# First attention: where GpSimd builds the second half's gate tables

## The chip, the cores and the metric

The kernel runs on one core of a Trainium2 chip. The metric is the device time of one execution in microseconds (us), smaller is better; the median of three runs is given.

## The reference, cut to what matters

The program is a two-layer block over 16 sequences (B) of 128 tokens (N) with 256 features. Layer 0 is a cross attention with 16 heads of 64 whose scores are weighted by a gate computed from boxes, then a ternary feed-forward layer. Layer 1 is a second cross attention, then a mixture of 8 experts with two experts per token. Only the first attention matters here:

```
emb = box_relational_embedding(boxes)            # sin and cos of 4 log distances x 2 frequencies
g   = relu(einsum('bnmd,hd->bhnm', emb, Wg) + bg)
a   = einsum('bhqd,bhkd->bhqk', q, k) / sqrt(64)
mn  = softmax(log(clip(g, 1e-6)) + a)
x   = x + tanh(g_xattn[0]) * (einsum('bhqk,bhkd->bqhd', mn, v) @ Wo.T + bo)
```

The x and y distances need a logarithm per pair of tokens (the "features"). The width and height distances are differences of logarithms, so their sines and cosines separate into a part of the query token times a part of the key token: those parts are the "gate tables".

## The kernel before, in words

All matmul operands are pairs of float16, a high half (rounded) and a low half (the rest), so that three products give nearly float32 results. ScalarE writes most high halves, GpSimd (POOL) most low halves by a subtraction, VectorE (DVE) does what reads PSUM.

The first attention is one loop over the 16 sequences, written out by hand for each engine as `iteration(b, ...)`, with semaphores between the engines. In iteration b each engine works on several sequences: the scores and gate of b, the projections of b + 1, the probability-times-value product, turn and output projection of b - 1, and the loads and split of b + 2. The order on an engine is the order in which its program is written; a wait holds everything behind it on that engine.

- **VectorE**, in iteration b: `norm` (L862) of b + 2; `row_max` (L873) and `take_qk` (L894); `take_pv` (L886); `feature_floor` (L846), `take_v` (L903), `feature_turns` (L851), `xn_low` (L867); `residual` (L909, L912); `feature_fractions` (L855, L857); `feature_distance` of b + 2 (L839, eight instructions, the last of which raises `s_fd`, called gate_difference, to b + 3); `probs` (L923, eight instructions: gate times exponentials into PT); and `bn_stats` (L1012).
- **ScalarE**: `probs_high` of b - 1 (L1419, four instructions, after all of `probs`), conversions, the logarithm (L1355), `take_o` (L1377), the negated expert weights (L1383), the exponentials (L1393), and the sine and its high half (L1362, L1366).
- **GpSimd**: `half_low(b - 1)` (L573, a DMA with accumulation that waits for ScalarE's L1383), `probs_low(b - 1)` (L560, four instructions, each after one of L1419), `feature_low` (L555), `split_qk` (L546, four), `half_high` (L569, a DMA), `split_v` (L551, two), `split_ctx` (L516, "the context's low half") and then, in some iterations, `separable`.
- **TensorE**: its product of probabilities and values (`pv`, L1766) waits for all four L560; later it turns the result, and `project_o` (L1786, float32) waits for L1377.
- **SyncE** queues the loads. At b = 8 `store_tables(1)` (L378, L379) waits for all eight GpSimd tables of the second half, writes them to DRAM and waits for that; `load_tables` (L388) reads a sequence's tables back.

`separable(g, j, base)` builds table part j (16 query tokens) of half g: two multiplications into Lp (L521), then a sum to float16 (L526), a sum in place (L528) and a subtraction (L530). Each of the last three waits for the one before it through `s_pp` (prefix_pool), and the helper ends with a wait for L530. Half 0 (sequences 0 to 7) is built before the loop. Half 1 is needed from sequence 8 on; before the change its eight parts are built at the end of iterations 0 (parts 0 and 1) and 1 to 6 (part b + 1).

Of the kernel before, what the change touches and what calls it, by code (L numbers as in the profile page):

```python
# [25 lines left out]
NJ = N // NN  # L26
# [43 lines left out]
def build(nc, a):  # L70
    with ExitStack() as ctx:
        def sem(name):
            return ctx.enter_context(nc.semaphore(name))
# [206 lines left out]
        s_fd, s_fv, s_fa, s_fhi, s_flo = (sem("gate_" + n) for n in ("difference", "vector", "scalar", "high", "low"))  # L280
# [11 lines left out]
        s_ts, s_tl = sem("tables_stored"), [sem("tables_loaded_even"), sem("tables_loaded_odd")]  # L292
# [211 lines left out]
        def _(gp):  # L504
            pc = Count(s_pp)
# [7 lines left out]
            def split_ctx(b, par):  # L513

                gp.wait_ge(s_ch, b + 1)
                nc.gpsimd.tensor_tensor(ctx16[:, par, 1, :, :], ctxf[:, par, :, :], ctx16[:, par, 0, :, :], ALU.subtract).then_inc(s_cl, 1)  # L516

            def separable(g, j, base):

                for r in range(2):  # L520
                    nc.gpsimd.tensor_tensor(Lp[:, r, :, :], AB[:, r, :].unsqueeze(2).to_broadcast([P, H, NN]),  # L521
                                            wht[:, r, g:g + 1, bass.ds(j * NN, NN)].to_broadcast([P, H, NN]), ALU.mult).then_inc(s_pp, 1)
                gp.wait_ge(s_pp, base + 2)
                high = Lw16[:, 0, bass.ds(j, 1), :].rearrange("p o (h n) -> p (o h) n", h=H)
                low = Lw16[:, 1, bass.ds(j, 1), :].rearrange("p o (h n) -> p (o h) n", h=H)
                nc.gpsimd.tensor_tensor(high, Lp[:, 0, :, :], Lp[:, 1, :, :], ALU.add).then_inc(s_pp, 1)  # L526
                gp.wait_ge(s_pp, base + 3)
                nc.gpsimd.tensor_tensor(Lp[:, 0, :, :], Lp[:, 0, :, :], Lp[:, 1, :, :], ALU.add).then_inc(s_pp, 1)  # L528
                gp.wait_ge(s_pp, base + 4)
                nc.gpsimd.tensor_tensor(low, Lp[:, 0, :, :], high, ALU.subtract).then_inc(s_pp, 1)  # L530
                gp.wait_ge(s_pp, base + 5)
# [9 lines left out]
            def split_qk(b, par):  # L541
                for r in range(4):
                    w, g = r // 2, r % 2
                    hi = q16[:, par, w, 0, HS * g:HS * g + HS, :]
                    gp.wait_ge(s_qh, 4 * b + r + 1)
                    nc.gpsimd.tensor_tensor(q16[:, par, w, 1, HS * g:HS * g + HS, :], qt[:, r, :, :], hi, ALU.subtract).then_inc(s_ql, 1)  # L546

            def split_v(b, par):
                for r in range(2):
                    gp.wait_ge(s_vh, 2 * b + r + 1)  # L550
                    nc.gpsimd.tensor_tensor(vv16[:, par, 1, 8 * r:8 * r + 8, 0:DK], vf[:, r, :, :], vv16[:, par, 0, 8 * r:8 * r + 8, 0:DK], ALU.subtract).then_inc(s_vl, 1)  # L551

            def feature_low(n, par):
                gp.wait_ge(s_fhi, n + 1)
                nc.gpsimd.tensor_tensor(F16s[:, par, 1, :], fs, F16s[:, par, 0, :], ALU.subtract).then_inc(s_flo, 1)  # L555

            def probs_low(c):
                for g in range(4):
                    gp.wait_ge(s_ph, 4 * c + g + 1)
                    nc.gpsimd.tensor_tensor(PT16[:, 1, HS * g:HS * g + HS, :], PT[:, HS * g:HS * g + HS, :],  # L560
                                            PT16[:, 0, HS * g:HS * g + HS, :], ALU.subtract).then_inc(s_pl, 1)

            def half_expert(h):
                return a["wcat"][h // 2, :, (h % 2) * HC:(h % 2 + 1) * HC]

            def half_high(h):
                if h > 1:
                    gp.wait_ge(w_ld[h % 2], h // 2 * 16)
                gp.dma_start(w16_dram.ap()[h // 2, :, 0, (h % 2) * HC:(h % 2 + 1) * HC], half_expert(h)).then_inc(w_hi[h % 2], 16)  # L569

            def half_low(h):
                gp.wait_ge(w_ng, h * NSP + NSP)
                gp.dma_start(wsp[:, h % 2, :], half_expert(h), accum_op=ALU.add, max_dma_last_dim=6144).then_inc(w_lo[h % 2], 16)  # L573
# [7 lines left out]
            def iteration(b, par, c, has_q, has_x, has_s=False):  # L581
                if c:
                    half_low(b - 1)
                    probs_low(b - 1)
                    feature_low(b, par)
                if has_q:
                    split_qk(b + 1, 1 - par)
                if has_x:
                    half_high(b + 2)
                if has_q:  # L590
                    split_v(b + 1, 1 - par)
                if has_x:
                    split_ctx(b + 2, par)
                if has_s:

                    if b == 0:
                        gp.wait_ge(s_ts, 96)
                        separable(1, 0, pc.n + 5 * NJ)
                    separable(1, b + 1, (b + 1) * 5 + (pc.n + 5 * NJ))

            iteration(0, 0, 0, True, True, True)

            iteration(1, 1, 1, True, True, True)
            for b in range(2, B - 2):
                iteration(b, b % 2, 2, True, True, b < NJ - 1)
            iteration(B - 2, 0, 2, True, False)
            iteration(B - 1, 1, 2, False, False)
            half_low(B - 1)
# [1613 lines left out]
```

## Time and profile before

| | us |
|---|---|
| median of 3 runs | 1168.07 |
| lowest and highest run | 1168.0 and 1172.73 |
| the profiled execution's own time | 1164.61 |
| its span (first to last instruction) | 1162.8 |
| mean granted TensorE clock, share of full speed | 0.925 |
| busy: PE / DVE / ACT / POOL | 955.3 / 836.2 / 689.7 / 718.9 |

The four engines are all busy for 59 to 82% of the span, and no one of them is the limit throughout: the chain of work that ended last runs through PE (51%), DVE (18%), POOL (14%) and ACT (6%). Shares of the whole span say nothing of one stage, so the first attention (until about 490 us) has to be read in its own stretch.

### The profile page before, as it was taken

How to read it: one execution, taken by the hardware profiler on the slowest of the kernel's cores; microseconds unless marked ns; L12 is line 12 of the kernel's file. 1: busy time of each engine (PE TensorE's matmuls, PEld its weight loads, DVE VectorE, ACT ScalarE, POOL GpSimd, SP SyncE). 2: the span in 40 equal slices, each digit the busy share in tenths (PEclk: the TensorE clock that was granted, in tenths of full speed). 3: DMA queues.
4: the chain of work that ended last, by engine and by line, in shares of the span. 5: the costliest groups of instructions: out<-in, count | busy, mean ns of one | idle time of the engine just before them, and what ended most of it. 6: DMA issues, size and time to landing. Idle time of an engine off the chain costs nothing.

```text
span 1162.8 us, 32870 instructions
## 1 busy us (share of the span) xinstructions
PE 955.3 (82%) x12178; PEld 779.8 (67%) x12178; DVE 836.2 (72%) x1947; ACT 689.7 (59%) x1338; POOL 718.9 (62%) x811
## 2 busy tenths in 40 slices
PE   0448988899999996387878559995599999999996
PEld 0336766667777764364554248873599999999995
DVE  3997888877887775657776779985566666666663
ACT  2456878888888884145425548884354545454542
POOL 2988778886677752115341539984566766666663
PEclk9888999999999997669999869995799999999998
DMA  9276667678776756330001000000555215841251
GB/s 277 72 192 142 122 129 146 150 167 183 140 149 154 154 105 148 98 130 1 1 14 41 19 2 16 26 21 19 201 142 140 32 32 140 246 142 32 32 144 16
DMA packets 52118, 119.65 MB, mean 103 GB/s; under 512 B 7617, under 2 KB 30145, under 8 KB 51633
## 3 DMA queue, kind: packets, MB, share of 16 engines
q0 software_dynamic: 14144, 35.48, 21.3%
q1 hardware_dynamic: 35520, 80.71, 20.7%
q10 hardware_dynamic: 2352, 2.10, 0.6%
q8 instruction: 66, 1.08, 0.4%
q14 instruction: 36, 0.29, 0.1%
HBM read 212.54 MB, written 37.85 MB: 215 GB/s over the span
## 4 chain that ended last, share of the span: by engine, by line
PE 51%; DVE 18%; POOL 14%; ACT 6%; issue 5%; DMA 4%; POOLq 0%; ACTq 0%; SPq 0%; DVEq 0%
PE bank L2107 17%; PE bank L2121 9%; POOL PT L560 6%; PE bank L1786 6%; PE bank L1689 3%; PE bank L1766 2%; DVE nmx L1177 2%; ACT EX L1393 2%; PE bank L1728 2%; DVE h L1063 2%; PE bank L1937 2%; PE bank L1721 1%; DVE PT L923 1%; PE bank L1780 1%; DMA gates<-in_g_ffn 1%
## 5 line engine op out<-in xcount | busy, mean ns | idle before, releaser
L1623 ACT ACTIVATE yg<-bank,bms 128x128 f32<-128x128 f32 x312 | 107.8, 364 | 106.8 <-PE bank L2107 98.9
L1296 DVE TENSOR_TENSOR hm<-hf,hm 128x256 f16<-128x256 f32 x156 | 70.3, 450 | 81.5 <-ACT hm L1630 81.5
L1291 DVE SCALAR_TENSOR_TENSOR hf<-bank,bms,yg 128x128 f32<-128x128 f32 x312 | 98.1, 345 | 33.2 <-ACT yg L1623 32.0
L2107 PE MATMUL bank<-xT,wm_even 128*128 128x128 f16 x1920 | 115.6, 221 | 1.0 <-DVE xT L1303 1.0
L2107 PEld LDWEIGHTS bank<-xT,wm_even 128*128 128x128 f16 x1920 | 111.5, 99 | 2.1 <-DVE xT L1303 1.4
L560 POOL TENSOR_TENSOR PT<-PT 128x512 f16<-128x512 f32 x64 | 72.7, 1183 | 61.4 <-ACT PT L1419 61.4
L707 POOL DMA_INDIRECT out_x<-ys,sidx x39 | 62.8, 1611 | 76.2 <-DVE ys L1310 76.2
L2107 PE MATMUL bank<-xT,wm_odd 128*128 128x128 f16 x1824 | 108.0, 219 | 1.8 <-DMA wm_odd<-expert_weights 1.8
L2107 PEld LDWEIGHTS bank<-xT,wm_odd 128*128 128x128 f16 x1824 | 104.2, 98 | 2.4 <-issue 1.9
L1630 ACT ACTIVATE hm<-hf 128x256 f16<-128x256 f32 x156 | 64.5, 414 | 63.1 <-DVE hf L1291 61.7
L619 POOL TENSOR_TENSOR h<-h 128x512 f16<-128x512 f32 x32 | 40.6, 1281 | 83.0 <-DVE h L1063 81.0
L546 POOL TENSOR_TENSOR q<-qt,q 128x512 f16<-128x512 f32 x64 | 80.0, 1299 | 0.8 <-ACT q L1406 0.7
L666 POOL TENSOR_TENSOR P<-P 128x512 f16<-128x512 f32 x64 | 72.9, 1171 | 11.4 <-ACT P L1579 11.4
L1786 PE MATMUL bank<-WoT,OT 128*128 128x256 f32 x256 | 64.5, 409 | 1.9 <-ACT OT L1377 1.9
L700 POOL DMA_INDIRECT xin<-expert_tokens,gidx x39 | 42.0, 1076 | 31.1 <-POOL b2r L722 25.5
L1786 PEld LDWEIGHTS bank<-WoT,OT 128*128 128x128 f32 x256 | 50.9, 204 | 13.3 <-ACT OT L1377 6.1
L1406 ACT ACTIVATE q<-qt 128x512 f16<-128x512 f32 x64 | 38.8, 625 | 33.8 <-DVE qt L894 33.8
L2121 PE MATMUL bank<-wm_even,hm 128*128 128x256 f16 x480 | 55.7, 273 | 2.0 <-DVE hm L1296 2.0
L717 POOL TENSOR_SCALAR gts<-xin,etf 128x1 f32<-128x1 f32 x78 | 56.3, 1091 | 0.7 <-DMA xin<-expert_tokens,gidx 0.6
L1766 PE MATMUL bank<-vv,PT 128*128 128x65 f16 x768 | 33.9, 200 | 26.4 <-POOL PT L560 15.6
L1747 PE MATMUL bank<-We,F16s 128*128 128x256 f16 x384 | 53.7, 276 | 0.0
L1689 PE MATMUL bank<-wqkv,ctx 128*128 128x512 f16 x192 | 48.1, 390 | 6.4 <-DVE qt L894 6.4
(308 smaller groups left out, 2646.7 us busy)
## 6 DMA issues: line engine op xcount, KB each, us to landing
wm_even<-expert_weights SPq DMA_DIRECT2D x60, 1024.0 KB
wm_odd<-expert_weights SPq DMA_DIRECT2D x57, 1024.0 KB
expert_weights<-in_wcat POOLq DMA_DIRECT2D x16, 768.0 KB, 7.8
wsp<-expert_weights SPq DMA_DIRECT2D x16, 768.0 KB, 4.4
wsp<-in_wcat POOLq DMA_DIRECT2D x16, 768.0 KB, 10.3
expert_weights<-wsp SPq DMA_DIRECT2D x16, 768.0 KB, 3.3
Lst<-gate_tables SPq DMA_DIRECT2D x48, 68.0 KB, 6.0
gate_tables<-Lw SPq DMA_DIRECT2D x6, 512.0 KB, 3.3
```

The costliest lines, as they stand in the source:

```text
L546: nc.gpsimd.tensor_tensor(q16[:, par, w, 1, HS * g:HS * g + HS, :], qt[:, r, :, :], hi, ALU.subtract).then_inc(s_ql, 1)
L560: nc.gpsimd.tensor_tensor(PT16[:, 1, HS * g:HS * g + HS, :], PT[:, HS * g:HS * g + HS, :], PT16[:, 0, HS * g:HS * g + HS, :], ALU.subtract ...
L666: nc.gpsimd.tensor_tensor(P116[:, b % 2, 1, HS * g:HS * g + HS, :], P1[:, b % 2, HS * g:HS * g + HS, :], P116[:, b % 2, 0, HS * g:HS * g + ...
L707: nc.gpsimd.indirect_dma_start(out=a["out"], out_offset=bass.IndirectOffsetOnAxis(ap=sidx[:, t:t + 1], axis=0), in_=ys[:, t % 2, :], in_of ...
L1291: v.scalar_tensor_tensor(hf[:, (c // 2) % 2, c % 2, :], bank[c % 4][:, MT:2 * MT], bms[:, par, FC + c:FC + c + 1], yg[:, c % 4, :], ALU.ad ...
L1296: v.tensor_tensor(hm16[:, par, 1, c - 1:c + 1, :], hf[:, q % 2, :, :], hm16[:, par, 0, c - 1:c + 1, :], ALU.subtract).then_inc(m_hl, 1)
L1623: s.activation(yg[:, c % 4, :], bank[c % 4][:, 0:MT], ACT.Gelu, bias=bms[:, par, c:c + 1]).then_inc(m_g, 1)
L1630: s.activation(hm16[:, par, 0, 2 * q:2 * q + 2, :], hf[:, q % 2, :, :], ACT.Copy).then_inc(m_hh, 1)
L1689: ins = t.matmul(bank[2 + r][:, :], ctx16[:, par, xp, kk, :], wqkv16[:, 2, wp, kk, 512 * r:512 * r + 512], start=(n == 0), stop=(n == 5))
L1786: ins = t.matmul(bank[7][:, 0:D], OT[:, ch, :], WoT[:, ch, :], start=(ch == 0), stop=(ch == CH - 1))
L2107: ins = t.matmul(bank[c % 4][:, w * MT:(w + 1) * MT], wm16[par][:, wp, col:col + P], xT16[:, par, xp * KD + kk, :], start=(n == 0), stop=( ...
L2121: ins = t.matmul(bank[5 + par][:, 0:D], hm16[:, par, xp, c, :], wm16[par][:, wp, col:col + D], start=(n == 0), stop=(n == 3 * FC - 1))
```

## The change

Table part b of the second half is now built in iteration b, not in iteration b - 1. In GpSimd's program it stands after `half_low(b - 1)` and before `probs_low(b - 1)`, and waits for `s_fd` to reach b + 2, which is VectorE's last `feature_distance` instruction of its iteration b - 1. Part 0 stays at the end of iteration 0. Nothing else is changed.

```diff
             def iteration(b, par, c, has_q, has_x, has_s=False):
                 if c:
                     half_low(b - 1)
+                    if has_s:
+                        gp.wait_ge(s_fd, b + 2)
+                        separable(1, b, b * 5 + (pc.n + 5 * NJ))
                     probs_low(b - 1)
                     feature_low(b, par)
...
                 if has_x:
                     split_ctx(b + 2, par)
-                if has_s:
-
-                    if b == 0:
-                        gp.wait_ge(s_ts, 96)
-                        separable(1, 0, pc.n + 5 * NJ)
-                    separable(1, b + 1, (b + 1) * 5 + (pc.n + 5 * NJ))
+                if has_s and b == 0:
+                    gp.wait_ge(s_ts, 96)
+                    separable(1, 0, pc.n + 5 * NJ)
...
             for b in range(2, B - 2):
-                iteration(b, b % 2, 2, True, True, b < NJ - 1)
+                iteration(b, b % 2, 2, True, True, b < NJ)
```

The instructions of PE, DVE, ACT and SP are the same and in the same order; only GpSimd's differ. At its border between iterations 0 and 1 (the first five rows removed are table part 1):

```order
-L521 TENSOR_TENSOR Lp<-AB,wht 128x256 [waits prefix_pool]
-L521 TENSOR_TENSOR Lp<-AB,wht 128x256
-L526 TENSOR_TENSOR Lw<-Lp 128x256 [waits prefix_pool]
-L528 TENSOR_TENSOR Lp<-Lp 128x256 [waits prefix_pool]
-L530 TENSOR_TENSOR Lw<-Lp,Lw 128x256 [waits prefix_pool]
 L573 DMA wsp<-in_wcat 128x2x1536 [waits half_expert_negated,prefix_pool]
-L560 TENSOR_TENSOR PT<-PT 128x512 [waits probs_high] x4
+L521 TENSOR_TENSOR Lp<-AB,wht 128x256 [waits gate_difference]
+L521 TENSOR_TENSOR Lp<-AB,wht 128x256
+L526 TENSOR_TENSOR Lw<-Lp 128x256 [waits prefix_pool]
+L528 TENSOR_TENSOR Lp<-Lp 128x256 [waits prefix_pool]
+L530 TENSOR_TENSOR Lw<-Lp,Lw 128x256 [waits prefix_pool]
```

The part moved from in front of the DMA L573 to behind it, and L560 now follows L530 instead of the DMA. At the later borders (iterations 1 to 6 into the next) GpSimd had before:

```order
L516 TENSOR_TENSOR ctx<-ctxf,ctx 128x256 [waits ctx_high]
L521 TENSOR_TENSOR Lp<-AB,wht 128x256 x2
L526 TENSOR_TENSOR Lw<-Lp 128x256 [waits prefix_pool]
L528 TENSOR_TENSOR Lp<-Lp 128x256 [waits prefix_pool]
L530 TENSOR_TENSOR Lw<-Lp,Lw 128x256 [waits prefix_pool]
L573 DMA wsp<-in_wcat 128x2x1536 [waits half_expert_negated,prefix_pool]
L560 TENSOR_TENSOR PT<-PT 128x512 [waits probs_high] x4
```

and has now:

```order
L516 TENSOR_TENSOR ctx<-ctxf,ctx 128x256 [waits ctx_high]
L573 DMA wsp<-in_wcat 128x2x1536 [waits half_expert_negated]
L521 TENSOR_TENSOR Lp<-AB,wht 128x256 [waits gate_difference]
L521 TENSOR_TENSOR Lp<-AB,wht 128x256
L526 TENSOR_TENSOR Lw<-Lp 128x256 [waits prefix_pool]
L528 TENSOR_TENSOR Lp<-Lp 128x256 [waits prefix_pool]
L530 TENSOR_TENSOR Lw<-Lp,Lw 128x256 [waits prefix_pool]
L560 TENSOR_TENSOR PT<-PT 128x512 [waits probs_high,prefix_pool]
L560 TENSOR_TENSOR PT<-PT 128x512 [waits probs_high] x3
```

Each part stands one DMA and one wait on VectorE later, directly ahead of the low halves of the probabilities; iteration 7, which built none before, now builds the last one.

## Rows read from the trace of the kernel before

**Rows 1.** The page's costliest groups: busy us, mean ns, then idle before.

```profile
L560 POOL TENSOR_TENSOR PT<-PT 128x512 f16<-128x512 f32 x64 | 72.7, 1183 | 61.4 <-ACT PT L1419 61.4
```

**Rows 2.** Windows from one L560 group's start to the next: length, busy, clock, DMA.

```profile
95.94:124.56 28.62, 23.33 (x277) 17.48 (x275) 20.83 (x43) 18.93 (x28) 19.17 (x21) 0.94 0.69 127
124.56:149.66 25.10, 23.40 (x309) 18.02 (x306) 20.27 (x44) 20.37 (x30) 20.79 (x19) 1.00 0.69 139
...
250.04:273.64 23.60, 21.79 (x279) 16.39 (x277) 19.26 (x45) 20.39 (x30) 16.26 (x14) 1.00 0.87 195
```

**Rows 3.** Timeline of VectorE, a 25.1 us iteration: start, length, instruction.

```profile
214.97 1.35 DVE L912 SCALAR_TENSOR_TENSOR X<-otmp,tg,X 128x256 f32<-128x256 f32 x1
...
221.46 2.73 DVE L923 SCALAR_TENSOR_TENSOR PT<-bank,EX 128x256 f32<-128x256 f32 x8
```

**Rows 4.** Timeline of GpSimd in the same iteration.

```profile
214.83 1.20 POOL L521 TENSOR_TENSOR Lp<-AB,wht 128x256 f32<-128x256 f32 x2
...
216.98 1.06 POOL L528 TENSOR_TENSOR Lp<-Lp 128x256 f32<-128x256 f32 x1
218.12 1.53 POOL L530 TENSOR_TENSOR Lw<-Lp,Lw 128x256 f16<-128x256 f32 x1
```

**Rows 5.** Timeline of VectorE in a 23.6 us iteration, which builds no table.

```profile
312.37 0.49 DVE L912 SCALAR_TENSOR_TENSOR X<-otmp,tg,X 128x256 f32<-128x256 f32 x1
...
316.87 2.74 DVE L923 SCALAR_TENSOR_TENSOR PT<-bank,EX 128x256 f32<-128x256 f32 x8
...
319.87 0.40 DVE L862 TENSOR_SCALAR xn<-X,mv,rstd 128x256 f32<-128x256 f32 x1
```

**Rows 6.** Timeline of GpSimd and ScalarE in the same iteration.

```profile
315.46 1.21 POOL L573 DMA_DIRECT2D wsp<-in_wcat  x1 [3.17 <-ACT wsp L1383]
320.15 1.13 ACT L1419 ACTIVATE PT<-PT 128x512 f16<-128x512 f32 x2
320.85 1.15 POOL L560 TENSOR_TENSOR PT<-PT 128x512 f16<-128x512 f32 x1 [4.19 <-ACT PT L1419]
```

**Rows 7.** Timeline of GpSimd at the border between iterations 0 and 1.

```profile
90.77 1.20 POOL L521 TENSOR_TENSOR Lp<-AB,wht 128x256 f32<-128x256 f32 x2
...
93.66 0.67 POOL L530 TENSOR_TENSOR Lw<-Lp,Lw 128x256 f16<-128x256 f32 x1
94.64 1.30 POOL L573 DMA_DIRECT2D wsp<-in_wcat  x1 [0.31 <-POOL Lw L530]
```

**Rows 8.** Timeline of VectorE at the same border.

```profile
90.69 2.07 DVE L923 SCALAR_TENSOR_TENSOR PT<-bank,EX 128x256 f32<-128x256 f32 x6
...
93.70 0.79 DVE L862 TENSOR_SCALAR xn<-X,mv,rstd 128x256 f32<-128x256 f32 x1
```

**Rows 9.** Timelines of VectorE and TensorE in iteration 1.

```profile
103.49 4.05 DVE L846 TENSOR_SCALAR fu<-fu 128x1024 f32<-128x1024 f32 x1
...
110.17 5.41 PE L1786 MATMUL bank<-WoT,OT 128*128 128x256 f32 x16
```

**Rows 10.** The same two instructions in a 23.6 us iteration.

```profile
304.78 0.74 DVE L846 TENSOR_SCALAR fu<-fu 128x1024 f32<-128x1024 f32 x1
...
308.15 3.72 PE L1786 MATMUL bank<-WoT,OT 128*128 128x256 f32 x16
```

**Rows 11.** Windows of iteration 1: columns as in rows 2.

```profile
105.00:110.00 5.00, 1.58 (x9) 0.59 (x6) 4.47 (x4) 2.43 (x4) 3.40 (x4) 1.00 0.73 206
110.00:115.00 5.00, 5.00 (x17) 3.96 (x16) 0.42 (x1) 4.29 (x7) 4.58 (x7) 0.66 1.00 264
```

**Rows 12.** Timeline of GpSimd before the loop, right behind table part 7 of half 0.

```profile
61.52 0.68 POOL L530 TENSOR_TENSOR Lw<-Lp,Lw 128x256 f16<-128x256 f32 x1
62.28 4.48 POOL L546 TENSOR_TENSOR q<-qt,q 128x512 f16<-128x512 f32 x4
```

**Rows 13.** Timeline of SyncE's queue: the stored tables and the first load.

```profile
244.78 0.33 SPq L378 DMA_DIRECT2D gate_tables<-Lw  x1
...
258.49 1.25 SPq L388 DMA_DIRECT2D Lst<-gate_tables  x3
```

## The prediction

> **What bounds the kernel now.** I read the page first. Its costliest groups say that GpSimd sat idle for 61.4 us ahead of L560, released by ScalarE's L1419 [rows 1]. So in the first attention GpSimd, over the loop, has time to spare, yet L560 is what TensorE's product of probabilities and values waits for. Its first instruction in each iteration is a good beat to count by. Second, I cut the loop into windows from beat to beat [rows 2]. There are three lengths: 28.62 us for iteration 1, then 25.10 five times over (the first is shown), then 23.60 from 250 us on. DVE is busy 20.27 us in a long one and 19.26 in a short one, and POOL 20.79 against 16.26. The long ones are those in which a gate table was built (five of them, after iteration 1). PE, ACT and the clock differ little, so the 1.50 us are no work of TensorE.
>
> Third, I set the timelines of a long and a short iteration side by side. In the long one VectorE needs 221.46 - 214.97 = 6.49 us from L912 to the start of L923 [rows 3]; in the short one 316.87 - 312.37 = 4.50 us [rows 5]. That is 1.99 us, and it begins with L912, 1.35 us in place of 0.49. It has inputs in SBUF and runs beside GpSimd's L521, whose last table step takes 1.53 us here [rows 4] and 0.67 elsewhere [rows 7]. Each engine holds the other up. L923 then starts late, L1419 waits for it, and L560 waits for L1419. In the short iteration VectorE's L923 ends before ScalarE is free (319.6 against 320.15) [rows 5, 6]: 0.5 us of the 1.99 had cover, and 1.5 show.
>
> **The change part by part.** *The old place is emptied.* In the five long iterations nothing of GpSimd runs beside L912 to L839, so they become short ones: 5 x (25.10 - 23.60) = 7.5 us. That is the firmest term, since the kernel itself shows the short iteration [rows 2].
>
> *The new place.* Seven tables (parts 1 to 7) now run behind L573 and behind the end of L839. In a short iteration L573 ends at 315.46 + 1.21 = 316.67, and L839 at the start of L923, 316.87 [rows 5, 6]. POOL's answer to a semaphore takes about 0.1 us, so a table starts at 316.97. Undisturbed it takes 93.66 + 0.67 - 90.77 = 3.56 us [rows 7] and ends at 320.53; the next instruction follows 0.08 us behind such an end [rows 12]. That is 320.61, and L560 starts at 320.85 anyway [rows 6]. It fits with 0.24 us to spare. L573 itself is issued earlier than in a long iteration and costs nothing: it ends ahead of the wait.
>
> What runs beside it? L923 first. Does it collide as L912 does? The border of iterations 0 and 1 already has this very pair: table part 1 at 90.77 beside L923 at 90.69 [rows 7, 8]. Six L923 take 2.07 us there, 0.33 from start to start, as do the eight in 2.74 [rows 5], and the table steps are at their shortest. So I take zero. The upper bound is the rate of the old place, 218.12 + 1.53 - 214.83 = 4.82 us for a table [rows 4]: 1.26 us more, of which 0.24 are covered, so 1.0 per iteration and 7 us in all. After L923 comes `norm` (L862, 319.87), which does collide: 0.79 us behind the same table against 0.40 [rows 5, 8]. If VectorE wins there, GpSimd's last step starts up to 0.4 late, L560 0.15 late, and seven times that is 1 us. If GpSimd wins, `norm` is 0.4 late, and its followers have slack because TensorE waits for L560. I take 0.3 us in all, between 0 and 1.
>
> The Trainium skill ("SBUF — State Buffer", Who interferes with whom) says that VectorE and GpSimd share a pair of ports under an exclusive lock, that a float32 `tensor_scalar` from SBUF to SBUF takes it, and that whoever issues first keeps it for its whole instruction. It speaks against this place: `norm` would hold the table up each time, and the sum would be that 1 us worse, no more.
>
> *Iteration 1.* This is the term that the reader may miss. Its 28.62 us hold two more delays: L846 takes 4.05 us against 0.74, and L1786 5.41 against 3.72 [rows 9, 10]. L846 starts 7.55 us after the beat (103.49 - 95.94), exactly as in the short iteration (304.78 - 297.25 = 7.53, that beat being 23.60 ahead of 320.85) [rows 6, 10], so it is not late; it is held 3.31 us by GpSimd's L546, running without a gap. Before it GpSimd ran from the DMA L573 straight into L560, with no wait between them: the DMA ends at 94.64 + 1.30 = 95.94, the beat [rows 7, 2]. Its queue ran ahead and stayed ahead. In the later iterations L560 begins after an idle wait [rows 6], and L846 gets through. Now L573 is followed by the table, whose steps wait for each other, and L560 starts behind a real wait. Behind a table L546 ran at its plain pace, four in 4.48 us [rows 12]. So I expect L846 near 0.74 us. TensorE then does not stand still: it was busy 1.58 of 5.00 us in 105 to 110, and only after that its granted clock fell to 0.66, a mix of its levels of 2.4 and 1.2 GHz [rows 11]. That cost L1786 its 1.69 us. Iteration 1 becomes a short one: 28.62 - 23.60 = 5.0 us. The lower bound is that the hold stays, gain 0; I take the 5.0, as the cause (no wait ahead of L560) goes with the edit.
>
> By the same section of the skill a blocked instruction waits for one instruction of the other engine, at most 1.1 us here. Row 9 shows 3.3 us, so the rule alone does not give what was measured. If the hold had a cause that the rule and I both miss, it stays, and the sum is 5.0 smaller.
>
> *The beat of iteration 1 itself.* Before: 95.94. Part 0 ends just ahead of 90.77. Now L573 starts 0.31 us behind it, at 91.0, and ends at 92.3 [rows 7]; the table ends at 95.9, and L560 starts 0.08 later. The same. But `norm` now meets the middle of the table: add 0.3 us.
>
> *SyncE.* Part 7 now ends just before the beat at 250.04 instead of 244.78, so storing the second half's tables starts some 5 us later, and the first load moves from 258.49 to about 263.5 [rows 13]. The gate of sequence 8 needs it two beats on, near 290. Free; if that cover were gone, it would cost up to 5 us once.
>
> **Sum:** 7.5 + 5.0 - 0.3 - 0.3 = 11.9 us. Against the profiled execution's own 1164.61 us (span 1162.8) that is 1152.7. The median of the runs shown, 1168.07, stands 3.5 us above that execution; I forecast the median, 1168.07 - 11.9 = 1156.2. What follows the attention shifts as a whole.
>
> **The rivals.** *B, only the old place gains (0.22).* The hold of L846 stays, because it is GpSimd's four L546 in a row that make it. For: in iteration 1 they ran gapless. Against: they do in the others too, with L846 at 0.74. Gain 7.5 - 0.6 = 6.9: 1161.2.
>
> *C, the collision only moves (0.13).* The table runs at the old place's 4.82 us, L560 is 1.0 late in seven iterations. For: the slack is only 0.24 us. Against: rows 7 and 8. Gain 11.9 - 7 = 4.9: 1163.2, no change by the bound below.
>
> *D, slower (0.06).* The hold of iteration 1 spreads. If a table ends after L1419 has released L560, GpSimd has ready work from the table to the last L546, and L846 waits 3.3 us in each of the seven iterations, with the fall of the clock 5.0. It decides as soon as the table ends later than 320.85. Six more such iterations cost 30 us, less the 7.5: 1168.07 + 22.5 = 1190.6. Against: the wait between L530 and L560 remains, and rows 12 show L546 at its plain pace behind just that wait.
>
> **How the numbers follow.** My forecast has 0.59, for 1154 to 1158 (one us either way for `norm`, one for the level of the runs). About 0.5% (5.8 us) is what a measurement of this kernel can tell from no change. Faster by more: the forecast and nearly all of B, 0.80. Same: C and the rest of B, 0.14. Slower: 0.06. The range takes in B and C and, below, a median nearer to the profiled execution's level: 1151.5 to 1163.5.
>
> **What would show it.** L912 near 0.49 us in all iterations; every beat-to-beat window 23.6 us, iteration 1 too; L846 0.74 there and L1786 3.7, with a clock of 1.00; tables of 3.6 us beside L923, ending within 0.3 us of L560's start. I am wrong if L923 or L1419 shifts later, if L560 follows a table without idle time in most iterations, or if iteration 1 keeps its 28.6 us.

## The result, and the profile after

The changed kernel takes 1161.08 us (median of 6 runs, 1156.32 to 1163.38), the kernel before 1168.7 (median of 6 runs beside it, 1168.0 to 1172.73). The ratio is 0.9906, with a 95% interval of 0.9888 to 0.9924: the change is 0.8 to 1.1% faster, 7.6 us by the medians. The forecast was 1156.2 with a range of 1151.5 to 1163.5: the median lies in the range, 4.9 us above the forecast, and the gain is 7.6 us where 11.9 were forecast. The profiled execution of the changed kernel took 1160.38 us, with a span of 1158.5 and a granted clock of 0.925 as before.

The page of the changed kernel has the row that answers to [rows 1]. L560's idle time behind L1419 fell from 61.4 to 42.7 us, since the table now stands in it; its 64 instructions cost the same.

```profile
PE 958.8 (83%) x12178; PEld 778.2 (67%) x12178; DVE 822.9 (71%) x1947; ACT 683.9 (59%) x1338; POOL 712.6 (62%) x811
...
L560 POOL TENSOR_TENSOR PT<-PT 128x512 f16<-128x512 f32 x64 | 72.3, 1158 | 42.7 <-ACT PT L1419 42.7
```

Busy time fell by 13.3 us on DVE and 6.3 on POOL: their instructions are the same, so they wait less inside them. The windows from beat to beat answer to [rows 2]; these are iterations 1, 2 and 7.

```profile
95.84:120.62 24.78, 23.14 (x307) 17.95 (x305) 19.75 (x44) 20.38 (x30) 19.75 (x19) 1.00 0.71 145
120.62:144.29 23.67, 22.61 (x294) 17.22 (x291) 19.23 (x44) 20.36 (x30) 19.60 (x20) 1.00 0.73 150
...
238.96:262.57 23.61, 22.56 (x293) 17.16 (x290) 19.16 (x45) 20.29 (x30) 16.27 (x15) 1.00 0.89 219
```

The five iterations of 25.10 us are now 23.66 to 23.68. Iteration 1 is 24.78 us, neither the old 28.62 nor the 23.60 that was forecast. The old length has to be set right first. The window of [rows 2] starts at 95.94, where the row of the transfer L573 ends, but GpSimd's timeline of the kernel before has L560 0.46 us earlier:

```profile
95.48 4.98 POOL L560 TENSOR_TENSOR PT<-PT 128x512 f16<-128x512 f32 x4
```

From start to start, as every other iteration is counted, the old iteration 1 lasts 124.56 - 95.48 = 29.08 us; that number is used from here on. The timelines of iteration 1 answer to [rows 3, 4, 9]: first VectorE, then GpSimd, then TensorE.

```profile
103.76 1.47 DVE L846 TENSOR_SCALAR fu<-fu 128x1024 f32<-128x1024 f32 x1
...
112.09 0.49 DVE L912 SCALAR_TENSOR_TENSOR X<-otmp,tg,X 128x256 f32<-128x256 f32 x1
...
114.48 2.13 DVE L839 TENSOR_SCALAR fu<-cm,cn,rw 128x128 f32<-128x128 f32 x8
116.59 2.74 DVE L923 SCALAR_TENSOR_TENSOR PT<-bank,EX 128x256 f32<-128x256 f32 x8
...
119.58 0.84 DVE L862 TENSOR_SCALAR xn<-X,mv,rstd 128x256 f32<-128x256 f32 x1
```

```profile
115.17 1.22 POOL L573 DMA_DIRECT2D wsp<-in_wcat  x1 [4.13 <-ACT wsp L1383]
116.70 1.19 POOL L521 TENSOR_TENSOR Lp<-AB,wht 128x256 f32<-128x256 f32 x2 [0.31 <-DVE fu L839]
...
119.60 0.67 POOL L530 TENSOR_TENSOR Lw<-Lp,Lw 128x256 f16<-128x256 f32 x1
120.62 4.51 POOL L560 TENSOR_TENSOR PT<-PT 128x512 f16<-128x512 f32 x4 [0.35 <-ACT PT L1419]
```

```profile
107.87 3.72 PE L1786 MATMUL bank<-WoT,OT 128*128 128x256 f32 x16
```

L912 is back at 0.49 us. The table starts 0.1 us behind L839's end (114.48 + 2.13 = 116.61), takes 119.60 + 0.67 - 116.70 = 3.57 us beside L923, and L923 keeps its 2.74. `norm` (L862) takes 0.84 us, the one collision left. L560 still starts behind an idle wait for L1419. L1786 is at 3.72, and the clock did not fall.

### The profile page after: what moved, and what is told of

Read it like the earlier page. It is cut to its first block, busy times and chain, and to the rows that moved or that the text cites. A ratio compares the mean times of both kernels' runs of the same rounds, so it can differ in the third digit from the quotient of the medians.

```text
span 1158.5 us, 32871 instructions
## 1 busy us (share of the span) xinstructions
PE 958.8 (83%) x12178; PEld 778.2 (67%) x12178; DVE 822.9 (71%) x1947; ACT 683.9 (59%) x1338; POOL 712.6 (62%) x811
## 4 chain that ended last, share of the span: by engine, by line
PE 51%; DVE 17%; POOL 11%; ACT 9%; issue 6%; DMA 4%; ACTq 0%; SPq 0%; POOLq 0%; DVEq 0%
PE bank L2107 17%; PE bank L2121 9%; POOL PT L560 5%; PE bank L1786 5%; PE bank L1689 3%; ACT EX L1393 2%; PE bank L1728 2%; PE bank L1766 2%; DVE h L1063 2%; DVE nmx L1177 2%; PE bank L1937 2%; ACT L1362 1%; PE bank L1721 1%; PE bank L1899 1%; ACT fks L1362 1%
## 5 line engine op out<-in xcount | busy, mean ns | idle before, releaser
L1296 DVE TENSOR_TENSOR hm<-hf,hm 128x256 f16<-128x256 f32 x156 | 66.8, 428 | 99.7 <-ACT hm L1630 94.2
L2107 PE MATMUL bank<-xT,wm_even 128*128 128x128 f16 x1920 | 117.7, 221 | 3.1 <-DVE hf L1291 1.8
L2107 PEld LDWEIGHTS bank<-xT,wm_even 128*128 128x128 f16 x1920 | 111.5, 99 | 6.2 <-DVE hf L1291 3.9
L2107 PE MATMUL bank<-xT,wm_odd 128*128 128x128 f16 x1824 | 110.1, 219 | 2.3 <-DVE hf L1291 2.3
L2107 PEld LDWEIGHTS bank<-xT,wm_odd 128*128 128x128 f16 x1824 | 104.2, 98 | 4.9 <-DVE hf L1291 2.4
L560 POOL TENSOR_TENSOR PT<-PT 128x512 f16<-128x512 f32 x64 | 72.3, 1158 | 42.7 <-ACT PT L1419 42.7
L1786 PE MATMUL bank<-WoT,OT 128*128 128x256 f32 x256 | 62.1, 398 | 1.9 <-ACT OT L1377 1.9
L1786 PEld LDWEIGHTS bank<-WoT,OT 128*128 128x128 f32 x256 | 49.2, 197 | 12.5 <-ACT OT L1377 6.0
L573 POOL DMA_DIRECT2D wsp<-in_wcat x16 | 19.6, 1222 | 57.1 <-ACT wsp L1383 56.7
```

The lines of the kernel that those rows point to most:

```text
L1296: v.tensor_tensor(hm16[:, par, 1, c - 1:c + 1, :], hf[:, q % 2, :, :], hm16[:, par, 0, c - 1:c + 1, :], ALU.subtract).then_inc(m_hl, 1)
L1786: ins = t.matmul(bank[7][:, 0:D], OT[:, ch, :], WoT[:, ch, :], start=(ch == 0), stop=(ch == CH - 1))
L2107: ins = t.matmul(bank[c % 4][:, w * MT:(w + 1) * MT], wm16[par][:, wp, col:col + P], xT16[:, par, xp * KD + kk, :], start=(n == 0), stop=( ...
```

## The experiments

Twelve runs were made: the two kernels again, eight other kernels, and two of these ten once more. The first eight runs were on one chip and the last four on another, and each is compared with the kernel before on its own chip. "Eighth beat" is the start of L560 in iteration 8, the end of the stretch that the change touches. In the traces that have lines added or taken out, a line number is off by one to seven from that of before; each is named. Where steps are added that count up `s_pp`, the count that `store_tables` waits for is raised to match; the diffs do not show that.

**The two kernels again.** No edit.

> The changed kernel once more, with a trace of its own. In the first trace the attention is 11 us ahead of the kernel before at the eighth beat and 12.8 us at the first matmul of the experts (814.6 against 827.4), and the end only 4.3 us. Theory 1 (the experts' loop runs at one of several paces that differ from execution to execution, whatever the kernel): the experts begin at 814 to 815 us again, and their length is something between 321 us (before) and 328 us (after), not the same as last time; beats of 23.6 to 23.7 us. Theory 2 (the change itself makes the experts slower): the experts take 328 us again, within 1 us.

> The kernel before once more, for its trace. In five traces of four other kernels the experts take 327 to 329 us from their first to their last matmul of the even tiles and a pair of tiles 16.9 us; only the first trace of the kernel before has 321 and 16.4. Theory 1 (two paces whatever the kernel, and the first trace caught the rarer one): 327 to 329 us now, a span of about 1169, and the attention as before: iteration 1 28.6 us, then five of 25.1. Theory 2 (the kernel before really has the faster experts): 321 us again.

Measured: the change 1160.7 us against 1170.76, ratio 0.9897 (0.9855 to 0.994). The kernel before, with one time beside its trace, 1171.04. This second trace of the kernel before corrects the first. Its iteration 1 lasts 26.05 us, not 29.08. GpSimd and VectorE in it:

```profile
94.45 1.32 POOL L573 DMA_DIRECT2D wsp<-in_wcat  x1 [0.31 <-POOL Lw L530]
96.09 4.51 POOL L560 TENSOR_TENSOR PT<-PT 128x512 f16<-128x512 f32 x4 [0.32 <-ACT PT L1419]
...
107.56 0.56 POOL L569 DMA_DIRECT2D expert_weights<-in_wcat  x1
108.13 2.22 POOL L551 TENSOR_TENSOR vv<-vf,vv 128x512 f16<-128x512 f32 x2
```

```profile
104.18 1.30 DVE L846 TENSOR_SCALAR fu<-fu 128x1024 f32<-128x1024 f32 x1
...
107.69 4.99 DVE L851 TENSOR_SCALAR fu<-fu,cst 128x1024 f32<-128x1024 f32 x1
```

This time L1419 came later than the transfer L573, so L560 did wait, and L846 got through in 1.30 us. Instead L851 was held: 4.99 us against the 0.81 it takes in the changed kernel's iteration 1. It started 0.13 us behind the transfer L569, and GpSimd went from that transfer into L551 without a pause. The hold is real, but in two executions of the same kernel it struck two instructions, at two prices. Nor is the changed kernel free of it: in iteration 0, ahead of the first beat, its L857 starts right behind a transfer L569 and takes 5.49 us in the first trace (5.34 and 5.15 in its other two) against 1.22. Between this trace of the kernel before and the change's own on the same chip the eighth beat moved from 271.20 to 262.30, 8.9 us: 0.5 before the first beat, 1.3 in iteration 1, and 7.2 in the five others (25.10 to 23.66).

**One half of the change at a time.** In the first kernel only part 1 is moved; parts 2 to 7 stay in the old place.

```diff
-                    if has_s:
+                    if b == 1:
                         gp.wait_ge(s_fd, b + 2)
                         separable(1, b, b * 5 + (pc.n + 5 * NJ))
...
+                if has_s and 0 < b < NJ - 1:
+                    separable(1, b + 1, (b + 1) * 5 + (pc.n + 5 * NJ))
```

> Only table part 1 is moved to the new place (iteration 1, behind L573 and the wait); parts 2 to 7 are built at the ends of iterations 1 to 6 as before. Theory 1 (the 28.6 us of iteration 1 came from L560 following the DMA with no wait between): iteration 1 takes 24.8 us as in the changed kernel, L846 about 1.5 us, L1786 3.7; the next five beats stay 25.1; the attention is 3.8 us ahead at the eighth beat. Theory 2 (iteration 1 was shortened by something else that the other moves did, such as the table that no longer runs at its end): iteration 1 keeps 28.6 us and nothing is gained.

The second is the other half: parts 0 and 1 in iteration 0, parts 2 to 7 in the new place.

```diff
-                    if has_s:
+                    if has_s and b > 1:
...
+                    separable(1, 1, 5 + (pc.n + 5 * NJ))
```

> Parts 0 and 1 are built at the end of iteration 0 as in the kernel before, and parts 2 to 7 in the new place. Theory 1: iteration 1 is held again, L846 4 us and L1786 5.4 us, 28.6 us from beat to beat; the next five beats take 23.66; the attention is 7.2 us ahead at the eighth beat. Theory 2 (iteration 1's gain belongs to the later moves): iteration 1 takes 24.8 us and all 11 us are there.

Measured: 1168.98 us for part 1 alone (ratio 0.9989, 0.9969 to 1.0009), 1162.17 for the rest alone (0.9933, 0.991 to 0.9955), with the kernel before at 1170.76 and the change at 1160.7 on the same chip. So by the medians the rest is worth 8.6 us, and part 1 is worth 1.8 by itself and 1.5 on top of the rest. The two halves measured apart add up, 8.6 + 1.8 = 10.4 against 10.1 together. But part 1's share is not clear of noise: the interval of its own ratio holds 1, and those of the rest alone and of the change overlap. With part 1 alone, all iterations to the sixth last 25.07 to 25.09 us, the first too, and its L848 (L846 of before) takes 0.74; its eighth beat, 269.41, is 4.2 us ahead of the first trace of before and 1.8 of the second. With the rest alone, L560 again follows the transfer directly, and the hold of [rows 9] is back. Its iteration 1, GpSimd, VectorE's L847 (L846 of before) and TensorE's L1656 and L1787 (L1655 and L1786) of that kernel:

```profile
94.87:122.31 27.44, 22.37 (x291) 17.01 (x288) 21.43 (x43) 19.58 (x29) 19.68 (x20) 1.00 0.74 137
```

```profile
94.03 1.30 POOL L573 DMA_DIRECT2D wsp<-in_wcat  x1 [0.31 <-POOL Lw L530]
94.87 4.98 POOL L560 TENSOR_TENSOR PT<-PT 128x512 f16<-128x512 f32 x4
```

```profile
102.87 4.05 DVE L847 TENSOR_SCALAR fu<-fu 128x1024 f32<-128x1024 f32 x1
```

```profile
109.16 0.41 PE L1656 MATMUL bank<-ident,xn 128*128 128x128 f32 x2 [3.42 <-ACT OT L1378]
109.56 3.72 PE L1787 MATMUL bank<-WoT,OT 128*128 128x256 f32 x16
```

The hold has the same 4.05 us and TensorE the same 3.42 us of idle time as in the trace of before, where its row also says 3.42; but L1787 took 3.72 us, not 5.41. The clock's fall does not come with the hold each time. This splits the old iteration 1: with the hold and a clock of 1.00 it lasts 27.44 us, 3.8 above a short one of 23.66, and with the clock's fall as well 29.08, 1.64 more, where L1786 alone took 1.69 more.

**The wait taken away.** The tables keep their new place and no longer wait for L839.

```diff
                     if has_s:
-                        gp.wait_ge(s_fd, b + 2)
                         separable(1, b, b * 5 + (pc.n + 5 * NJ))
```

> The change without its wait for VectorE's distances: each table starts right behind the DMA L573. The tables do not read what the wait is for, so nothing else is changed. Theory 1 (GpSimd's steps and VectorE's instructions with SBUF inputs hold each other up, so the wait is worth having): the first steps now run beside L839, L839's eight take 2.5 us or more in place of 2.13 in iterations 2 to 7; since VectorE has 0.5 us of cover the beat grows by 0 to 0.3 us to at most 23.9, and GpSimd's table ends earlier by up to 0.3 us. In all 0 to 2 us slower than with the wait. Theory 2 (it is the place behind the DMA that matters, and the wait is idle decoration): beats the same 23.66 us within 0.03, and L839 at 2.13.

Measured: 1178.58 us, ratio 1.005 (1.0026 to 1.0074), 17.9 us behind the change. No theory had that size. Window, GpSimd and VectorE of one iteration (L838 and L850 are L839 and L851 of before):

```profile
177.05:204.71 27.66, 24.05 (x293) 18.82 (x292) 25.56 (x44) 20.42 (x30) 19.42 (x20) 0.93 0.62 128
```

```profile
196.36 1.22 POOL L573 DMA_DIRECT2D wsp<-in_wcat  x1 [4.46 <-ACT wsp L1382]
197.17 1.64 POOL L521 TENSOR_TENSOR Lp<-AB,wht 128x256 f32<-128x256 f32 x2
```

```profile
188.52 3.94 DVE L850 TENSOR_SCALAR fu<-fu,cst 128x1024 f32<-128x1024 f32 x1
...
195.67 5.58 DVE L838 TENSOR_SCALAR fu<-cm,cn,rw 128x128 f32<-128x128 f32 x8
```

The table begins 1.5 us behind L839's start, while it runs, and L839 takes 5.58 us in place of 2.13 (4.12 in the iteration of 25.09 us); L923 starts that much later. L851, 0.02 us behind the transfer L569, is held as well, 3.94 us, and three of the iterations last 27.7 us. Why L851 falls there in this kernel was not followed. The wait, which I had priced at nothing, is the most valuable line of the change.

**The same delay by other means.** Here GpSimd waits for a one-column memset of its own instead of for VectorE.

```diff
+            def fenced(done):
+                pc.up(nc.gpsimd.memset(fence[:, :], 0.0))
+                gp.wait_ge(s_pp, pc.n + 5 * NJ + 5 * done)
...
-                        gp.wait_ge(s_fd, b + 2)
+                        fenced(b)
```

> The change with its wait for the distances replaced by a wait for a one-column memset of GpSimd's own, between the DMA L573 and the table. The table may then start ahead of VectorE's L839, but it no longer follows the DMA without a wait. Theory 1 (the 27.7 us iterations without a wait come from GpSimd running ahead behind its DMA, which keeps VectorE out until GpSimd first waits): L839's eight take under 3 us, L851 is not held, beats of 23.7 to 24.3 us, the whole at most 4 us slower than the change. Theory 2 (a table beside L839 costs that much in any case): L839's eight 4 us and more, beats above 26 us, the whole 15 us and more slower than the change.

Measured: 1159.2 us against 1171.61 beside it, ratio 0.9896 (0.9868 to 0.9924), level with the change. L574, L583 and L522 are the transfer L573, the memset and the table's L521; L844 is L839.

```profile
208.44 1.22 POOL L574 DMA_DIRECT2D wsp<-in_wcat  x1 [3.17 <-ACT wsp L1388]
209.23 0.67 POOL L583 MEMSET fence<- 128x1 f32 x1
209.99 1.20 POOL L522 TENSOR_TENSOR Lp<-AB,wht 128x256 f32<-128x256 f32 x2
```

```profile
207.74 2.14 DVE L844 TENSOR_SCALAR fu<-cm,cn,rw 128x128 f32<-128x128 f32 x8
```

At that point two readings were open. Either a wait between GpSimd's transfer and its next work frees VectorE, or all that counts is that the table starts behind L839: 207.74 + 2.14 = 209.88, and the table starts at 209.99, exactly as with the change. The next two kernels tell these apart. In the first, the memset stands there without a wait for it (the line `gp.wait_ge(s_pp, ...)` above is left out).

> Edit: the one-column memset stands between the transfer L573 and the table, and GpSimd does not wait for it. The table's steps start some 0.3 to 0.6 us later than without it, and nothing breaks GpSimd's run. Theory 1 (a wait between the transfer and the table is what frees VectorE): no gain over the run without the wait, 27 to 28 us per iteration, 1175 to 1180 us. Theory 2 (only the table's start against L839's end counts): with the start moved to L839's end the iterations fall to 23.7 to 25 us, and the time to 1160 to 1168 us.

In the second, the table stands ahead of the transfer, behind a wait for L857, the instruction just before L839.

```diff
-                    half_low(b - 1)
                     if has_s:
-                        gp.wait_ge(s_fd, b + 2)
+                        gp.wait_ge(s_fv, 4 * b + 4)
                         separable(1, b, b * 5 + (pc.n + 5 * NJ))
+                    half_low(b - 1)
```

> Edit: the seven tables stand ahead of the transfer L573 instead of behind it, behind a wait for VectorE's L857, the instruction just before L839; so each table starts at about the start of L839's eight instructions, behind a wait and not behind a transfer. Theory 1 (what holds VectorE is GpSimd's unbroken run behind its own transfer; a table beside L839 costs a plain collision): L839 grows from 2.13 to 3.5 us at most, the iterations take 24 to 25.1 us, and the run stands 2 to 9 us behind the change. Theory 2 (any table step that runs beside L839's short instructions holds them back for good, with or without a transfer): L839 takes 5 us or more as in the run without the wait, the iterations take 27 us or more, and the run stands 15 to 25 us behind the change.

Measured: 1167.84 us (ratio 1.0024, 1.0005 to 1.0043) without the wait, and 1167.16 (1.0012, 0.9989 to 1.0034) with the table inside L839, against 1155.35 for the change and 1163.99 for the kernel before on that chip. GpSimd and VectorE without the wait (L574, L583, L522 as above; L843 is L839):

```profile
192.99 1.22 POOL L574 DMA_DIRECT2D wsp<-in_wcat  x1 [3.17 <-ACT wsp L1387]
193.77 0.55 POOL L583 MEMSET fence<- 128x1 f32 x1
193.83 1.63 POOL L522 TENSOR_TENSOR Lp<-AB,wht 128x256 f32<-128x256 f32 x2
```

```profile
192.29 4.87 DVE L843 TENSOR_SCALAR fu<-cm,cn,rw 128x128 f32<-128x128 f32 x8
```

The memset alone did not move the table's start, 0.84 us behind the transfer's: it ran inside the end of the transfer's instruction. So this kernel did not shift what it was made to shift, and it is a second run of the table beside L839, with 25.84 us per iteration. The kernel with the table ahead of the transfer (its lines are those of before) has the clean case, a table that starts 0.16 us behind L839's start, behind a real wait and behind no transfer:

```profile
194.41 1.24 POOL L521 TENSOR_TENSOR Lp<-AB,wht 128x256 f32<-128x256 f32 x2 [2.63 <-DVE fu L857]
```

```profile
194.25 4.35 DVE L839 TENSOR_SCALAR fu<-cm,cn,rw 128x128 f32<-128x128 f32 x8
...
L839 DVE TENSOR_SCALAR fu<-cm,cn,rw x8: 334/651/886, 194.2 to 198.3; 128x128 f32<-128x128 f32 x8
```

```profile
95.52:126.25 30.73, 24.73 (x302) 18.83 (x300) 22.96 (x43) 19.52 (x29) 19.70 (x21) 0.94 0.61 119
126.25:151.50 25.25, 22.66 (x294) 17.22 (x292) 20.90 (x44) 20.50 (x30) 19.60 (x19) 1.00 0.66 139
```

The second row of VectorE gives the shortest, middle and longest of the eight in ns. Undisturbed, eight take 2.13 us, 0.27 from one start to the next; here the middle one takes 0.65, and GpSimd's steps stand 0.8 us apart. VectorE gets one short instruction in per step of the table. That costs 2.2 us on VectorE and 1.6 per iteration (25.25 against 23.66). So the second reading holds for the steady iterations: what counts is that no table step stands beside L839, and the wait's virtue is that it puts the table behind it. The first reading keeps iteration 1: with nothing between the transfer and L560 there, L846 took 4.05 us again, L1786 5.41, and the iteration 30.73. The run stands 11.8 us behind the change, outside what either theory had (2 to 9, and 15 to 25). Theory 1 fits the steady iterations, whose five times 1.6 us are 8 us, though L839 passed its 3.5; it had no price for the hold in iteration 1, which as a whole lasts 7.1 us more than the change's 23.67 on that chip.

The Trainium skill ("SBUF — State Buffer", Who interferes with whom) gives a blocked instruction a wait for one whole instruction of the other engine. For the eight L839 the trace agrees with it: each waits for one step anew, so a row of short instructions pays again and again. For L846 at 4.05 us it does not, as the prediction noted: one instruction stood through several of GpSimd's, which take 1.1 to 1.3 us each.

**A longer table.** Two more steps behind each moved table, with a wait for each, to use up the slack ahead of L560.

```diff
+                        for k in range(2):
+                            pc.up(nc.gpsimd.tensor_tensor(Lp[:, 1, :, :], Lp[:, 0, :, :], Lp[:, 0, :, :], ALU.add))
+                            gp.wait_ge(s_pp, pc.n + 5 * NJ + 5 * (b + 1))
```

> The change with two more steps behind each of the seven moved tables (a sum into a part of Lp that is overwritten, each with its own wait, about 0.8 us each). Theory 1 (the place has 0.35 us of idle time behind the table, and what goes beyond it is paid once per iteration, with no hold of L846): beats of 23.66 + 1.6 - 0.35 = 24.9 us in iterations 2 to 6, L846 at 0.74 to 1.5, 7 to 9 us slower than the change in all. Theory 2 (my rival D: once the table ends after L1419 has released L560, GpSimd runs on without a gap and L846 is held): L846 at 4 us, beats above 27 us, 25 us slower and more.

Measured: 1172.44 us against 1171.61, ratio 1.0012 (1.0001 to 1.0023), so all of the gain is gone, 11.7 us behind the change's 1160.7 where theory 1 had 7 to 9. GpSimd (L588 are the added steps) and VectorE's L849 (L846 of before):

```profile
171.83 1.31 POOL L588 TENSOR_TENSOR Lp<-Lp 128x256 f32<-128x256 f32 x2
173.21 4.51 POOL L560 TENSOR_TENSOR PT<-PT 128x512 f16<-128x512 f32 x4
```

```profile
180.96 1.63 DVE L849 TENSOR_SCALAR fu<-fu 128x1024 f32<-128x1024 f32 x1
```

1.38 us of added work cost 1.1 us per iteration, which fits a slack of about 0.3; iterations 2 and 4 take 26.0 us, at a granted clock of 0.93, and the first beat comes 2 us later. These are what theory 1 missed. L560 now follows the table with no wait, the condition of rival D. L846 takes 1.63 us, not the 4.05 that D needs: behind a table the long hold does not come. The change's trace on the second chip, below, has the same condition in iteration 1, with L846 at 0.74.

**The kernel before, with a wait ahead of L560 in iteration 1.** The memset and its wait between L573 and L560, there alone.

```diff
                     half_low(b - 1)
+                    if b == 1:
+                        fenced(2)
```

> The kernel before with one thing added: in iteration 1, between the DMA L573 and the first L560, a one-column memset of GpSimd and a wait for it. Theory 1 (L560 following the DMA with no wait is what makes the hold of L846 in iteration 1): L846 0.74 to 1.5 us, iteration 1 23.6 to 25.2 us, and the attention 3.3 to 5 us ahead of the kernel before at the eighth beat, though no table was moved. Theory 2 (the hold comes from something else): L846 at 4.05, iteration 1 27.4 us or more.

Measured: 1171.04 us, ratio 1.0002 (0.9991 to 1.0014). Iteration 1 lasts 25.08 us, like its neighbours, and L853 (L846) takes 0.74. But in iteration 0 the hold fell on L864 (L857), 5.15 us against 1.22, the first beat came at 98.20, and L561 (L560) waited 1.82 us for ScalarE, so it would not have followed the transfer directly without the memset either. What iteration 1 gained the late beat took back, and as to the cause this run decides nothing.

**The fence and the change side by side.** No new edit.

> Edit: the run with GpSimd's own memset and a wait for it in place of the wait for VectorE, once more, beside the change on one chip. If iteration 1 at 23.65 us instead of 24.78 is a property of this order, it comes again and the run stands 0.5 to 2 us ahead of the change; if it is one execution's draw, the two stand within 1 us of each other.

> The change itself once more, beside the run before. Iterations of 23.66 us from the third on, iteration 1 at 24.8 us if that is its habit; 1158 to 1162 us. In the experts' half, 16.9 us from one pair of tiles to the next if that is the usual pace, 16.4 if the quicker pace of the first trace of before is drawn by chance.

Measured: the fence 1153.96 us (1152.8 to 1156.72, ratio 0.9918), the change 1155.35 (1150.06 to 1158.3, ratio 0.9912, 0.9884 to 0.994), the kernel before 1163.99. The intervals overlap: no version here is shown to beat the change. And the lengths of iteration 1 changed places: the fence, 23.65 before, has 24.78 now, and the change, 24.78 and 24.77 before, has this:

```profile
96.30:119.97 23.67, 22.70 (x296) 17.35 (x294) 18.84 (x43) 20.02 (x30) 19.58 (x19) 1.00 0.76 153
```

```profile
95.55 0.67 POOL L530 TENSOR_TENSOR Lw<-Lp,Lw 128x256 f16<-128x256 f32 x1
96.30 4.51 POOL L560 TENSOR_TENSOR PT<-PT 128x512 f16<-128x512 f32 x4
```

That is the short iteration 1 of the forecast, with L846 at 0.74. (Where L846 takes 1.45 to 1.47, as in the change's other two traces and the fence's second, the iteration has 24.8.) So both kernels, the change and the fence, have shown 23.7 and 24.8 us: the length differs from execution to execution, and the kernel does not settle it. The kernel before has 26.05 or 29.08 in its two traces. The change also came in below its 1158 to 1162, and the kernel before is faster here too.

## Why the gain at the end differs from trace to trace

In the first pair of traces the experts' half begins 12.8 us earlier after the change and the span ends only 4.3 us earlier. I looked for something that the change does to the experts and found nothing. TensorE's first and last L2107 on `wm_even`, from the first trace of before, from that of after, and from the change on the one chip and on the other:

```profile
L2107 PE MATMUL bank<-xT,wm_even x1920: 219/219/314, 827.4 to 1148.5; 128*128 128x128 f16 x192
```

```profile
L2107 PE MATMUL bank<-xT,wm_even x1920: 219/219/314, 814.6 to 1142.5; 128*128 128x128 f16 x192
```

```profile
L2107 PE MATMUL bank<-xT,wm_even x1920: 219/219/314, 814.3 to 1143.0; 128*128 128x128 f16 x192
```

```profile
L2107 PE MATMUL bank<-xT,wm_even x1920: 219/219/314, 816.1 to 1138.8; 128*128 128x128 f16 x192
```

They last 321.1, 327.9, 328.7 and 322.7 us. One and the same kernel has both lengths. The change's second trace repeated its 328, as theory 2 on that run had it, but the second trace of the kernel before then lasted 327.5 (825.7 to 1153.2), so it is not the change that slows the experts. All eight traces of the first chip lie between 326.7 and 330.2, whatever the kernel, and all four of the second between 322.7 and 323.0. In these twelve the pace goes with the chip, and the kernel before is faster on the second as well (1163.99 against 1170.76). On which chip the first pair of traces was taken is not on record, so their 321.1 and 327.9 can't be put down to it. What sets the pace is open.

## Why the prediction was right, and where it was off

The mechanism of its largest term was right and so was that term's size. The second term, iteration 1, was too large by some 3 us, and the range held in spite of it.

- *The old place is emptied: 7.5 us.* Right. Five iterations fell from 25.10 to 23.66, 5 x 1.44 = 7.2 us, and the rest alone was worth 8.6 by its median. L912 is at 0.49 us. One reading under it was wrong: in [rows 2] PE is busy 23.40 us in a long iteration and 21.79 in a short one, which is 1.61 us and not "little". The conclusion held all the same, since TensorE's program did not change and the iterations fell. In the window of iteration 2 after the change PE has 22.61 busy us and 294 instructions, where the long one had 309.
- *The new place: L923 does not collide, `norm` does; 0.3 us.* Right. L923 keeps 2.74, `norm` takes 0.84, and the iteration is 0.06 us over the short one of [rows 2], 0.4 us over seven. The slack ahead of L560 was 0.24 by the sum and about 0.3 by the longer table; the trace shows 0.35 us of waiting there.
- *Iteration 1: 5.0 us.* This is the term that was mis-sized. "28.62 - 23.60 = 5.0" took one execution for the rule. It also counted from the end of the transfer's row: from L560's start the same execution has 29.08 - 23.60 = 5.5 us, and L846 started 8.01 us behind the beat, not 7.55, so it was 0.5 us late as well as held. The mechanism, L560 directly behind the transfer and then L846 held, is borne out: in all three traces in which L560 did follow the transfer at once (the first of before, the rest alone, the table inside L839) L846 took 4.05 us in iteration 1, and in the eleven others, with a wait or a table between them, 0.73 to 1.47. But the second trace of the same kernel had the wait by chance, with 26.05 us, and its hold on L851 instead. Part 1 is worth 1.5 to 1.8 us by the medians, within the noise of their difference. The clock's fall, 1.69 us of the term, came in two of those three traces only.
- *The beat of iteration 1: 0.3 us later.* It came at 95.84 against 95.48, 0.36 us later. That the number fits is luck: the beat varies from 95.63 to 96.30 in three traces of the change and from 95.48 to 96.09 in two of the kernel before.
- *SyncE's tables are free.* Right: the row that answers to the first of [rows 13] stands at 238.63, 23.9 us ahead of the eighth beat at 262.57, where it was 28.9 ahead (273.64 - 244.78). It is the 5 us later that were forecast, and the next iteration still takes 23.61. But the first load did not follow: it was forecast some 5 us later against its beat, at 263.5, and stands at 248.29, 9.3 us behind the beat at 238.96 where it was 8.5 behind (258.49 - 250.04). SyncE waited 5.6 us for the stored tables there, in place of 10.4; why is not followed.
- *Sum.* Against the trace that the forecast was worked out from, the stretch to the eighth beat gains 273.64 - 262.57 = 11.1 us, close to the 11.9. By one chip's two traces it gains 8.9 us, and the medians differ by 7.6, 10.1 and 8.6. The forecast took one trace's stretch off a median of runs, and that trace was typical in neither half: it had the quicker pace in the experts and the longer iteration 1. "What follows the attention shifts as a whole" did not hold in that pair, where 12.8 us at the first expert became 4.3 at the end.
- *The rivals.* B's number, 1161.2, met the time, but not B's reason: the hold of L846 did go, it was merely worth less. C fell, as the tables run at 3.57 us. D's condition was made by hand with the longer table, and its hold did not come. The slower outcome lay elsewhere: in leaving out the wait for L839, to which the prediction gave no price, and without which the kernel is 0.3 to 0.7% slower than before.

## What to carry to other kernels

When work is moved to GpSimd's idle time, place it by what VectorE does there: beside instructions that read PSUM it cost nothing here, beside one SBUF instruction 0.4 us, and beside eight short SBUF instructions 2.0 to 3.5 us. A wait for the other engine's last SBUF instruction was here no cost but the point of the move. And before a term is built on one odd iteration, look whether a second execution of the same kernel has it.

## What the runs showed of the hardware

- Eight 0.27 us VectorE instructions beside the steps of a GpSimd table get in at one per step, 0.65 us in the middle and 0.8 from step to step.
- One VectorE instruction can be held over several of GpSimd's: L846 4.05 us (0.74 undisturbed), L851 3.86 to 4.99 (0.81 to 1.03), L857 5.15 to 5.49 (1.22). L846 ended within 0.1 us of the end of GpSimd's unbroken run (107.54 against 107.63 in the first trace of before). In each case GpSimd had gone from its own transfer instruction into ready vector work without a pause. That this is the cause rests on order alone: in iteration 1 L846 was held in all three traces in which L560 followed the transfer L573 at once, and in none of the eleven others. No run isolates it.
- GpSimd's next instruction, if ready, starts 0.8 us after the transfer L573 does, although that one is shown with 1.2 to 1.3 us: a memset without a wait fits in there and delays the table by 0.03 us at most.
- The same 3.42 us pause of TensorE in iteration 1 was followed by a fall of its granted clock in two traces and by none in a third.
- The same kernel's experts' half lasted 328.7 us on one chip and 322.7 on another.
